# A third 512-column subtraction on ScalarE, and GpSimd's row transfers behind a slot's last subtraction

## The reference, cut to what matters

```python
xn = _layernorm(x)
# attention
q, k, v = split(xn @ w_attn)                     # 16 heads of 8
scores = q @ k.T / sqrt(8) + causal - log1p(decay[h] * log1p(dist))
y = softmax(scores) @ v
a = y @ w_proj
# experts
probs = softmax(xn @ Wr.T)                       # 8 experts, the best 2, gates of sum 1
f = sum over the 2 of gate * (silu(xn @ W1[e].T) @ W2[e].T)
return x + a + f
```

## Time and profile before

| | before |
|---|---|
| median of 3 runs | 574.65 us (573.76 to 575.19) |
| the profiled execution: its time, its span | 580.15 us, 578.4 us |
| TensorE busy | 517.7 us, 90% |
| GpSimd busy | 371.5 us, 64% |
| VectorE busy | 352.7 us, 61% |
| ScalarE busy | 320.7 us, 55% |
| granted TensorE clock, mean of the span | 0.955 |

### The profile page before, as it was taken

The page is one execution under the profiler, slowest core; times in us unless marked ns, Lnnn a source line. Parts: engine busy times, 40 slices in busy tenths (PEclk is TensorE's granted clock), DMA queues, the critical chain, the costliest instruction groups (busy, mean ns, idle before and its releaser), DMA issues.

```text
span 578.4 us, 13697 instructions
## 1 busy us (share of the span) xinstructions
PE 517.7 (90%) x4472; PEld 370.1 (64%) x4472; DVE 352.7 (61%) x1418; ACT 320.7 (55%) x569; POOL 371.5 (64%) x610
## 2 busy tenths in 40 slices
PE   3589999999999989999999989989999999999930
PEld 1477565565555555565555555545699999999930
DVE  5875898779866766776776676666133333333326
ACT  3656776767776666766776677556523333233300
POOL 3354576467787888788678888888245455554434
PEclk9757999999999999999999999999999999999975
DMA  6553673331430350350241243044546666766439
GB/s 164 164 176 104 189 153 110 111 103 46 134 89 15 121 159 15 98 174 20 83 143 46 70 126 105 16 148 117 134 135 203 210 194 203 221 197 202 145 122 326
DMA packets 69715, 76.49 MB, mean 132 GB/s; under 512 B 8318, under 2 KB 52352, under 8 KB 69648
## 3 DMA queue, kind: packets, MB, share of 16 engines
q1 hardware_dynamic: 65328, 67.16, 39.7%
q0 software_dynamic: 4320, 8.47, 4.3%
HBM read 46.16 MB, written 29.89 MB: 131 GB/s over the span
## 4 chain that ended last, share of the span: by engine, by line
PE 69%; POOL 15%; DVE 6%; issue 3%; DMA 3%; ACT 1%; SPq 1%; another core or an unknown queue 0%; DVEq 0%; POOLq 0%
PE psT L1176 20%; PE ps L1224 11%; PE psT L1251 11%; PE psO L1190 10%; POOL scores L671 8%; POOL rows_dram L682 7%; PE ps L1152 6%; DVE scores L1013 3%; PE psM L1129 3%; PE psM L1082 2%; PE psO L1101 2%; PE psM L1208 1%; DVE x_all L489 1%; PE ps L1215 1%; PE psM L1135 1%
## 5 line engine op out<-in xcount | busy, mean ns | idle before, releaser
L1013 DVE CUSTOM_DVE_ANT_0 scores<-ps,wdist 128x256 f32<-128x256 f32 (+3 forms) x512 | 222.2, 486 | 92.1 <-PE ps L1152 66.3
L671 POOL TENSOR_SCALAR scores<-scores,row_max 128x384 f32<-128x384 f32 (+2 forms) x448 | 221.5, 509 | 77.2 <-DVE row_max L1013 76.0
L776 ACT ACTIVATE probs<-psT 128x512 f32<-128x512 f32 x320 | 175.5, 596 | 80.8 <-PE psT L1176 78.5
L1176 PE MATMUL psT<-ident,scores 128*128 128x128 f32 x1280 | 179.3, 282 | 16.8 <-POOL scores L671 10.9
L1176 PEld LDWEIGHTS psT<-ident,scores 128*128 128x128 f32 x1280 | 138.3, 142 | 57.0 <-POOL scores L671 28.3
L689 POOL DMA_INDIRECT picked_dram<-scores,row_ring x71 | 69.7, 982 | 79.1 <-issue 42.9
L1190 PE MATMUL psO<-probs,values 128*32 128x512 f32 (+3 forms) x1024 | 94.9, 444 | 0.0
L794 ACT ACTIVATE scores<-ps 128x512 f32<-128x512 f32 x71 | 42.4, 597 | 94.1 <-PE ps L1224 94.1
L1224 PE MATMUL ps<-scores,wdist 128*128 128x128 f32 x568 | 75.2, 275 | 1.6 <-issue 1.0
L1251 PE MATMUL psT<-wdist,scores 128*128 x568 | 75.2, 275 | 0.3 <-ACT scores L794 0.3
L682 POOL DMA_INDIRECT rows_dram<-xn_all x64 | 62.8, 981 | 16.2 <-issue 16.2
(11 more groups left out here) (130 smaller groups left out, 322.9 us busy)
## 6 DMA issues: line engine op xcount, KB each, us to landing
wdist<-w1t SPq DMA_DIRECT2D x71, 256.0 KB
k_rows<-k_dram SPq DMA_DIRECT2D x64, 96.0 KB, 3.0
q_rows<-q_dram SPq DMA_DIRECT2D x64, 96.0 KB, 2.5
row_ring<-rows_dram SPq DMA_DIRECT2D x71, 65.0 KB
probs<-picked_dram SPq DMA_DIRECT2D x8, 512.0 KB, 6.8
rows_dram<-row_ring SPq DMA_DIRECT2D x7, 585.0 KB, 5.4
k_dram<-k_parts SPq DMA_DIRECT2D x8, 384.0 KB
q_dram<-q_parts SPq DMA_DIRECT2D x8, 384.0 KB
```

The costliest lines, as they stand in the source:

```text
L671: last = nc.gpsimd.tensor_scalar(part, part, -1.0, row_max[:, r, tile, quad:quad + 1], ALU.mult, ALU.add)
L776: nc.scalar.activation(probs[:, at.ring(2), w, :], psT[:, w % 2], ACT.Exp, scale=-1.0).then_inc(exp_ready, 1)
L1013: last = nc.vector.tensor_tensor_reduce(out=scores[:, r, u, col:col + n], in0=bank[:, col:col + n], in1=wdist[:, at.g * QUADS + quad, SEQ ...
L1176: last = nc.tensor.transpose(psT[:, w % 2, place * P:(place + 1) * P], scores[:, at.ring(2), u, col + key * P:col + (key + 1) * P], ident[:])
```

## The change

Unit 6, the first 512-column unit of the second two heads, goes from GpSimd to ScalarE. ScalarE subtracts it in a second `SA` step near the end of the slot, behind the exponentials of the last two blocks of the group before. The step `SC` with the row transfers goes from the middle of a slot, where it stood ahead of `P1` step 2, to behind that second `SA`; on GpSimd, which has no part in `SA`, that is behind the units 8 and 9 of `P1` step 4. TensorE's waits are counted anew for the three units of ScalarE and the seven of GpSimd.

```diff
-ACT_UNITS = 2
+ACT_UNITS = (0, 1, 6)
+POOL_UNITS = tuple(u for u in range(UNITS) if u not in ACT_UNITS)
...
-    step("SA", n, NGROUP)
+    step("SA", n, NGROUP, (0, 1))
...
-    pick = int(n > SECOND_PICK_SLOT)
-    first = SENDS * (n - (SECOND_PICK_SLOT + 1 if pick else FIRST_SEND_SLOT))
-    if 0 <= first < NTILE:
-        steps.append(("SC", 0, pick, first, min(NTILE, first + SENDS)))
     if n < FILLS:
         steps.append(("FL", 0, n))
     p1(2)
...
     p1(4)
     step("TE", n - 1, NGROUP, 8, 10)
+    step("SA", n, NGROUP, (6,))
+    pick = int(n > SECOND_PICK_SLOT)
+    first = SENDS * (n - (SECOND_PICK_SLOT + 1 if pick else FIRST_SEND_SLOT))
+    if 0 <= first < NTILE:
+        steps.append(("SC", 0, pick, first, min(NTILE, first + SENDS)))
...
                 def less_step(at, i):
-                    if i == 0:
-                        return
                     r = at.ring(2)
                     for strip in range(2):
                         u = 2 * i + strip
+                        if u in ACT_UNITS:
+                            continue
...
-                def less_act_step(at):
+                def less_act_step(at, units):
...
-                    for u in range(ACT_UNITS):
+                    for u in units:
                         act.wait_ge(p1_free, at.groups(UNITS, u + 1))
-                        part = scores[:, r, u, :]
-                        nc.scalar.activation(part, part, ACT.Identity, scale=-1.0, bias=row_max[:, r, TILES - 1, u:u + 1]
-                                             ).then_inc(less_act, 1)
+                        part, pair = scores[:, r, u, :], u // (UNITS // 2)
+                        quad = 2 * pair + u % 2
+                        nc.scalar.activation(part, part, ACT.Identity, scale=-1.0,
+                                             bias=row_max[:, r, TILES - 1, quad:quad + 1]).then_inc(less_act, 1)
...
-                        pe.wait_ge(less_max, at.groups(UNITS - ACT_UNITS, 4 if pair == 0 else 8))
-                        pe.wait_ge(less_act, at.groups(ACT_UNITS, ACT_UNITS))
+                        ready = (6, UNITS)[pair]
+                        pe.wait_ge(less_max, at.groups(len(POOL_UNITS), sum(u < ready for u in POOL_UNITS)))
+                        pe.wait_ge(less_act, at.groups(len(ACT_UNITS), sum(u < ready for u in ACT_UNITS)))
```

## The result

| | before | changed kernel |
|---|---|---|
| median | 574.65 us | 559.17 us (558.90 to 559.24, 3 runs) |
| ratio | | 0.9733, 95% interval 0.9714 to 0.9752 |
| profiled execution: its time, its span | 580.15 us, 578.4 us | 558.9 us, 557.2 us |

The change saves 15.5 us, 2.7%. The forecast was a saving of 10.7 us and a time of 564.0 us, with 557.5 to 573.0 as range: sign and range hold, the size was a third too small, and the time is that of the first rival (558.9). In a second set of runs the two kernels took 573.66 and 559.14 us, ratio 0.9738 (0.9717 to 0.976).

The account below looks back on a forecast made before the run. TensorE, busy 90%, was taken to lose 0.87 us a slot waiting for GpSimd behind row transfers. Terms -16.5 + 5.1 + 0.75 = -10.7 us, off the 574.65 us median: 564.0 us, range 557.5 to 573.0.

Parts of the forecast that it names:

- first rival: Slots with transfers: TensorE's signals cost nothing in the transfers' new place; 558.9 us, chance 0.22.
- The wait on L671: Attention slots with transfers: TensorE no longer waits for GpSimd's subtractions; -0.87 us in each of 19 slots, -16.5 us.
- Late signals: Start of the next slot: third transfer delays TensorE's signals, so exponentials and next transposes come late; 0.27 us a slot, +5.1 us.
- The tail: Slots 31 and 32: five transfers in one row end later, so the first expert transposes start later; +0.75 us.
- ScalarE's subtraction at nothing: Slot end on ScalarE: the moved 0.66 us subtraction of unit 6 is hidden in 0.76 us of idle time; no cost.
- The second pass: Slot 21: VectorE's wait for the first 32 transfers before rewriting rows is once, under a microsecond, covered by idle time; nothing.
- no price for late signals: Slots with transfers: signals fall between the transpose pairs, so only -16.5 and +0.75 us count; 558.9 us, chance 0.22.
- held rival: Start of the next slot: transposes are held 1.69 us too, costing +13.4 instead of +5.1 us; 572.3 us, chance 0.14.
- the one with ScalarE: ScalarE pays for the moved subtraction: 0.28 us uncovered in 31 slots, 8.7 us; 572.7 us, chance 0.07.
- the slower: A score matmul is held too, making VectorE's units and transfers late; 1.55 us a slot, 588.4 us, chance 0.08.
- the one without effect: The wait before a group's first transposes stays, held by exponentials instead of GpSimd; 574.7 us, chance 0.04.

Follow-up runs that it names:

- second profiled execution of before: The kernel before, profiled once more without an edit: 576.23 us, span 574.5 us.
- changed kernel's second execution: The changed kernel run and profiled again without an edit, in a second set of runs: median 559.14 us, ratio 0.9738 to the kernel before.

## Why the prediction was right, and where its terms were off

**The wait on L671** was the right mechanism, at the right place. Its size, 0.87 us for 19 slots or 16.5 us, was too large. The stretches of the second profiled execution of before and of the changed kernel, slots 10 to 30, measure it:

```profile
148.21:389.19 240.98, 227.50 (x2054) 137.51 (x2050) 172.59 (x744) 166.21 (x301) 202.28 (x351) 1.00 0.32 94
```

```profile
147.56:374.02 226.46, 226.46 (x2052) 137.51 (x2050) 171.90 (x744) 179.00 (x322) 186.31 (x330) 1.00 0.33 98
```

The difference is 14.5 us. The step that failed is to put the whole difference between the earlier trace rows down to GpSimd, as if all four slots waited for it. One in four, the slot with the projection, has over a microsecond more ahead of its first pair and never waited (11.83 us before and after); its 0.76 us came from the late signals of that execution. The others were 0.95 us longer each: there are 13 such slots (slot 21 has no transfers), 12.3 us, and slots 10 and 11 with 1.2 and 1.0 us make the 14.5. The stretch that served as a measure was not quite clean either: slots 6 to 9, 43.95 us in the earlier trace rows, take 43.69 us in the changed kernel.

**Late signals**, +5.1 us, measured zero: there are none in either profiled execution of the changed kernel. The rows did show them, and the place computed for them is right for such an execution; the step that failed is to carry one execution's behaviour to a median of others. There was a sign for it: the profiled execution took 580.15 us, 5.5 us above the median, and I scaled it away as 1% of everything. The Trainium skill, "SBUF — State Buffer", section "Who interferes with whom", states that PE and ACT never wait on anyone. By that rule this term was zero, and twelve of the thirteen profiled executions agree; whether for the page's reason, no run shows, since what held the signals in the one, up to 1.76 us, was not found.

**The tail**, +0.75 us, measured 0.04: from slot 31's start to the first expert 18.45 us, 18.41 in the second execution of before. In the changed kernel's second execution it is 18.72 us, so 0.3 us. The five transfers end 15.2 us into the slot, as worked out (15.1). But I took the 4.10 us from the last transfer to the expert for the time that the rows need; in the changed kernel, where TensorE really waits for them, it is 3.2 us (389.24 to 392.47). Before, TensorE came to it at 412.35 without a wait.

**ScalarE's subtraction at nothing** held: 573.69 us with it alone, and a second one free as well. **The second pass** at nothing held in the changed kernel, and four transfers a slot showed what that wait costs once it is not covered, 3.5 us.

**Left over** is about 0.65 us ahead of slot 10 (148.21 against 147.56): slots 1, 4 and 6 are shorter by 0.26, 0.34 and 0.27 us, and the first of them starts 0.27 us later. The 0.34 us of slot 4 is of that one execution of before (in the first it took 10.84 us, as in the changed kernel). The 0.27 us of slot 6 stands in every kernel with unit 6 on ScalarE and in none with it on GpSimd; why is not known. The prediction had expected nothing from slots 0 to 9. The sum of the measured parts, 14.5 + 0.65 - 0.04 = 15.1, is close to the 15.5 of the medians. The two spans compared differ by more, 17.3 us; the other 2.1 us lie behind the first expert (166.80 against 164.73 us), where the two kernels have the same work.

The rivals: *no price for late signals* came true in its time, but not for the reason that it gave, signals that fall between the pairs; there were no late signals. That its 558.9 us meets the 559.17 so closely is partly luck: its wait is 2.0 us too large, and the tail, the slots ahead of 10 and a part that was not located make up for it. The forecast itself was saved by its range: one term 2.0 us too large and one of 5.1 us that was not there stood against each other. The held rival, the one with ScalarE, the slower and the one without effect did not come about.

## What to carry to other kernels

Here it decided ahead of which instruction an engine's long chores stand, and not how much it has to do: GpSimd's load fell by 0.7 us a slot for nothing, while moving 3.7 us of transfers behind the units that TensorE wants next won 14.5 us in slots 10 to 30. The load counted only where GpSimd had no slack left, at the end of the attention slots. Before a term is worked out from something odd in a trace, compare that execution's time with the others of the same kernel; if it is longer by about what the oddity costs (here 5.5 and 4.8 us), profile again. And where several slots are averaged, look whether each shows the wait.

## What the runs showed of the hardware

- TensorE's granted clock fell from 1.00 to 0.50 near the end of an idle time of 2.88 us (for 6.80 us) and 0.6 and 1.1 us after the end of ones of 1.86 and 1.41 us (for 3.40 us each), where it had been busy before. After 1.13, 1.25 and 1.29 us of waiting for the rows, in the changed kernel, in the one with unit 7 on ScalarE and in the one with the transfers behind unit 7, it stayed at 1.00. By estimate, 3.40 us at half the clock cost 1.7 us of TensorE's work, about the length of the wait again.
- In one of thirteen profiled executions, consumers took TensorE's results up to 1.8 us late (203.58 against 201.18 + 0.64) beside a run of three indirect DMAs; in the attention slots of the others, with the same DMAs at the same place or elsewhere, never.
- Three indirect DMAs in a row kept GpSimd for 3.7 us: 1.02 us for the first, 0.96 for each other, 0.15 to 0.30 us ahead of each (200.28 to 203.83 in slot 14 of the changed kernel).
